# A mixture-of-experts kernel: transposes in the free quarter of the gate's PSUM bank, and down projections over two banks

## The reference

```
logits = normed @ router_w.T;  probs = softmax(logits);  top_v, top_i = top_k(probs, 2)
gates = softmax(top_v);  comb = sum over both of one_hot(top_i, 8) * gates
for e in range(8):
    gate, up = split(normed @ gate_up_w[e].T, 2)          # 384 columns each
    out = out + comb[:, e] * ((silu(gate) * up) @ down_w[e].T)
out = out + swiglu(normed, shared weights)                # 128 columns
```

## Time and profile before

| | |
|---|---|
| three runs | 674.36 us median (671.52 to 675.77) |
| profiled execution, span of the core | 674.1 us |
| profiled execution's own time | not given apart from the span; the span is 0.3 us under the median |
| mean granted TensorE clock | 0.926 |
| PE busy | 527.7 us (78%) |
| DVE, POOL and ACT busy | 391.4, 353.9 and 337.5 us |
| idle time of PE before parts 3, 0 and 1 | 36.4, 31.3 and 1.5 us |

### The profile page before, as it was taken

One profiled execution on the slowest core, in us unless ns is written; L12 is line 12 of the kernel. 1 busy time (PEld: TensorE's weight loads), 2 busy tenths in 40 slices (PEclk: granted clock), 3 DMA queues, 4 the chain that ended last, 5 costly groups with the idle time before them and its releaser, 6 DMA issues.

```text
span 674.1 us, 15456 instructions
## 1 busy us (share of the span) xinstructions
PE 527.7 (78%) x3928; PEld 472.9 (70%) x3928; DVE 391.4 (58%) x1785; ACT 337.5 (50%) x816; POOL 353.9 (52%) x515
## 2 busy tenths in 40 slices
PE   3756888787789998978896259696789887899882
PEld 2535777677778897867784258676578777899872
DVE  5576655531164886974894768678768351222454
ACT  3534444363344876744865158474554463454431
POOL 1445556565664346555274704546567666555332
PEclk9878999999998999999997669988699898999987
DMA  6915545465575454663220453411354665676894
GB/s 199 301 33 189 187 161 191 160 232 190 197 266 186 173 185 154 224 209 133 99 91 33 121 172 113 152 72 67 133 178 160 214 187 194 229 247 226 284 303 148
DMA packets 88019, 117.88 MB, mean 175 GB/s; under 512 B 11848, under 2 KB 60880, under 8 KB 87936
## 3 DMA queue, kind: packets, MB, share of 16 engines
q1 hardware_dynamic: 76208, 96.75, 42.6%
q0 software_dynamic: 9312, 19.16, 8.2%
q10 hardware_dynamic: 2416, 0.99, 0.6%
HBM read 26.57 MB, written 26.19 MB: 78 GB/s over the span
## 4 chain that ended last, share of the span: by engine, by line
PE 43%; issue 13%; DVE 12%; ACT 10%; another core or an unknown queue 9%; DMA 4%; POOL 4%; SPq 2%; ACTq 1%; DVEq 1%; POOLq 0%
PE ps_y L731 10%; PE ps_g L717 8%; PE ps_h L722 5%; PE ps_u L722 4%; DVE xres L1307 2%; PE w L629 2%; PE w L659 2%; PE ps_x L711 2%; PE w L660 2%; POOL rows L1539 2%; DMA xin<-rows 2%; PE w L615 1%; ACT zz L844 1%; PE w L675 1%
## 5 line engine op out<-in xcount | busy, mean ns | idle before, releaser
L1567 POOL DMA_INDIRECT results<-raw_gu,idx x163 | 159.6, 979 | 188.2 <-ACT raw_gu L940 127.2
L731 PE MATMUL ps_y<-dn_t,raw_gu 128*128 x978 | 145.9, 287 | 36.4 <-ACT raw_gu L940 27.0
L731 PEld LDWEIGHTS ps_y<-dn_t,raw_gu 128*128 128x128 f32 x978 | 126.2, 197 | 48.1 <-issue 47.0
L1539 POOL DMA_INDIRECT rows<-zz,s_idx x128 | 125.4, 979 | 42.6 <-issue 34.1
L717 PE MATMUL ps_g<-x_t,raw_dn 128*128 128x128 f32 x978 | 141.9, 283 | 1.5 <-issue 1.5
L717 PEld LDWEIGHTS ps_g<-x_t,raw_dn 128*128 128x128 f32 x978 | 127.5, 199 | 3.6 <-issue 3.4
L940 ACT COPY raw_gu<-ps_y 128x128 f32<-128x128 f32 x163 | 42.9, 263 | 148.1 <-PE ps_y L731 70.2
L1380 DVE TENSOR_TENSOR raw_gu<-sil,ps_u 128x384 f32<-128x384 f32 x82 | 45.2, 551 | 91.3 <-PE ps_u L722 26.6
L934 ACT ACTIVATE sil<-ps_g 128x384 f32<-128x384 f32 x163 | 80.0, 491 | 35.7 <-PE ps_g L717 17.8
L930 ACT ACTIVATE x_t<-ps_x,bf_c,gf_c 128x128 f32<-128x128 f32 x163 | 75.3, 462 | 42.6 <-PE ps_x L711 32.3
L1380 DVE TENSOR_TENSOR raw_gu<-sil,ps_h 128x384 f32<-128x384 f32 x81 | 44.7, 552 | 84.5 <-PE ps_h L722 27.5
(11 more groups left out here) (166 smaller groups left out, 747.4 us busy)
## 6 DMA issues: line engine op xcount, KB each, us to landing
raw_dn<-gu_t SPq DMA_DIRECT2D x163, 384.0 KB
xin<-rows SPq DMA_DIRECT2D x163, 64.5 KB
yg<-results SPq DMA_DIRECT2D x15, 512.0 KB
results<-raw_gu,idx POOLq DMA_INDIRECT x163
rows<-pads SPq DMA_DIRECT2D x40, 64.5 KB
rows<-pads SPq DMA_DIRECT2D x5, 451.5 KB
rows<-zz,s_idx POOLq DMA_INDIRECT x128
out<-xres SPq DMA_DIRECT2D x7, 256.0 KB
```

Of the source, the lines that this page charges most:

```text
L731: t = pe.matmul(ps_y[:, 0, :], h_t[:, k4, c * P:(c + 1) * P], dn[:, bass.ds(off + c * D, D)], start=(c == 0), stop=(c == FC - 1))
L1539: pool.indirect_dma_start(xs, bass.IndirectOffsetOnAxis(s_idx[n][:, c, k:k + 1], 0), zz[n][:, k, c, :], None).then_inc(scat[n], 16)
L1567: pool.indirect_dma_start(yt, bass.IndirectOffsetOnAxis(idx[:, ky:ky + 1], 0), yb[:, ky, :], None).then_inc(yst[ky], 16)
```

## The change

The bank `ps_x` is gone, and a second bank for the down projection takes its place. A block's rows are turned into the fourth quarter (`FC` is 3) of the bank that its gate projection uses later. The transpose therefore waits until the silu of block B-2 has read that bank, and the gate projection no longer has that wait itself. The down projection alternates between `ps_y0` and `ps_y1`, and waits for the copy of block B-2's where it waited for that of block B-1. The order of parts and the woven counts are as before. The banks that the weights are turned through at the start keep their order.

```diff
-        ps_x, ps_y = bank("ps_x"), bank("ps_y")
+        ps_y0, ps_y1 = ps_ys = bank("ps_y0"), bank("ps_y1")
         w0, w1 = bank("w0"), bank("w1")
-        weight_banks = ps_g[0], ps_u, ps_h, ps_x, ps_y, ps_g[1]
+        weight_banks = ps_g[0], ps_u, ps_h, ps_y0, ps_y1, ps_g[1]
...
-                    pe.wait_ge(xT_sb, B + 3)
+                    pe.wait_ge(sil_done, B + 3)
                     pe.wait_ge(xin_ld[k4], (B - k4) * 4 + 16)
-                    pe.transpose(ps_x[:, 0, :], xin[:, k4, 0:D], ident[:]).then_inc(xT_ps, 1)
+                    pe.transpose(ps_g[k][:, FC, :], xin[:, k4, 0:D], ident[:]).then_inc(xT_ps, 1)
                 elif part == 1:
                     pe.wait_ge(xT_sb, B + 4)
-                    pe.wait_ge(sil_done, B + 3)
                     pe.wait_ge(ws_ld[k4], (B - k4) * 4 + 16)
...
                     pe.wait_ge(h_done, B + 6)
-                    pe.wait_ge(y_sb, B + 6)
+                    pe.wait_ge(y_sb, B + 5)
...
-                        t = pe.matmul(ps_y[:, 0, :], h_t[:, k4, c * P:(c + 1) * P], dn[:, bass.ds(off + c * D, D)],
+                        t = pe.matmul(ps_ys[k][:, 0, :], h_t[:, k4, c * P:(c + 1) * P], dn[:, bass.ds(off + c * D, D)],
...
-                    act.activation(x_t[:, k, :], ps_x[:, 0, :], ACT.Identity, bias=bf_c[:], scale=gf_c[:]).then_inc(xT_sb, 1)
+                    act.activation(x_t[:, k, :], ps_g[k][:, FC, :], ACT.Identity, bias=bf_c[:], scale=gf_c[:]).then_inc(xT_sb, 1)
...
-                    act.copy(yb[:, ky, :], ps_y[:, 0, :]).then_inc(y_sb, 1)
+                    act.copy(yb[:, ky, :], ps_ys[k][:, 0, :]).then_inc(y_sb, 1)
```

## The result

The changed kernel takes 683.49 us (median of 4 runs, 681.2 to 686.26), the kernel before 673.83 (median of 4, 671.52 to 675.77). The ratio is 1.0165, with a 95% interval from 1.012 to 1.021: slower by 1.65%, some 10 to 11 us. The profiled execution took 686.26 us, its span is 684.4.

The account below looks back on a forecast made before the run. PE was taken to lead, busy 78% of the span, yet standing still about 146 us. The sum was 674.4 - 9.5 + 13.4 = 678.3, with half a microsecond for POOL's side 679 us; range 664 to 693.

Parts of the forecast that it names:

- forecast A: Whole kernel: gain and loss nearly cancel, the loss a little larger; 672 to 684 us, 679 in the middle; chance 0.45.
- Part 2: Transposes moved into the gate's bank wait for the silu of two blocks back: 13.4 us lost, bounds 0 to 29.5.
- step (b): Late silus before transposes up to 125 us: PE's gaps for other work hide the lateness, taking 12.1 us off the loss.
- Part 1: Two banks for the down projections, each waiting for an earlier block's copy: 9.5 us gained, bounds 0 to 36.4.
- C: Rival, faster: down projection stalls go and the transpose's wait stays hidden; 660 to 667 us; chance 0.17.
- B: Rival, slower: the transposes' silu waits are not absorbed, attention stages wait behind them; +20 us, 694; chance 0.28.
- D: Rival, nothing changes: the waits on PE only change their name; 674.4 us; chance 0.07.
- E: Rival, the clock: longer stops before transposes put 20 us of PE's work at the lower clock; 689 us; chance 0.03.
- Waits for ACT before D: Sign: PE's down projections' waits for ACT's copy of the result should fall from 27.0 to under 8 us.
- T(27) right behind S(25): Sign: PE's transpose of block 27 should follow ACT's silu of block 25 at once.
- The limit for B: Sign of the not-absorbed rival: idle times before down projections and transposes together growing by over 12 us.
- POOL's half microsecond: POOL's copying of row numbers after later transposes: half a microsecond added to the sum.

Follow-up runs that it names:

- its own control: Kernel before, with the silu reading a weight tile in SBUF in place of the gate's result, all waits as they were: ratio 0.9987.

## Why the prediction was right, and where it was not

**The sign and the place were right.** I gave 679 us; it is 683.5, at the upper edge of forecast A (672 to 684), and the range of 664 to 693 holds it. Slower by over 1% had 0.40, and no change that can be told had 0.44, so the outcome was not the one that I had given most. The loss is the wait of the transpose for the silu.

**Part 2, the cost: right in size.** The sum had 13.4 us. The pair that differs in this wait alone gives 1.75%, 12 us, 5 us uncertain. In detail the steps did less well. Silu waits were to be 20 to 35 us and are 42.2. Of step (b), that all lateness up to 125 us is covered, the profile shows no more than a part: T(2) waited 4.1 us, and T(6) starts 7.4 us late, 4.3 of it behind the late start of T(0). Later gaps cover more than I had counted, the wait of T(85) for its rows above all. That the steps miss and the sum fits is in part luck.

**Part 1, the gain: this step was not borne out.** "I take 9.5, the count by rows" is the term that looks mis-sized. With T's old wait it measured nothing, 0.4% slower with 0.6% uncertainty, beside its own control. There T's wait for X took 13.7 us of the idle time back, since X stands on ACT behind the same copies; I had not expected that, and had expected 9.5 us or more. In the change itself T waits for the silu, behind that X on ACT, and what the bank gave there is open: 0.6% of gain against the kernel with the transpose moved alone, 0.9% uncertain, which is 4 us and leaves room for 0 and for 9.5. With 0 in place of 9.5 the sum is 674.4 + 13.4 = 687.8; with the 12 us measured it is 686.4, 3 us above the median.

**The rivals.** C, faster with T's wait hidden, gave 664.9; with the wait truly gone the kernel came to 1.003 of before, 676 us by that ratio. So even its best case was not there. B said that the loss would not be absorbed, 694; it was absorbed about as far as the sum of 13.4 had it. D, that the waits only change their name, is right for part 1 where T kept its old wait. E, the clock: the mean granted clock fell from 0.926 to 0.902, but PE's busy time rose by 2.4 us only. PE's busy time moved by 5.8 us between two kernels with the same matmuls (both banks and the old wait beside its control), which is the size of a term, and had none in my sum; that the clock makes it is not shown.

**What was named as signs.** Waits for ACT before D under 8 us: 1.3. Idle time before T of 50 or more: 76.6. G's idle time near 1.5: 1.0. PE busy at 528: 530.1. T(27) right behind S(25), T(21) behind the table load: both, by 0.06 and 0.05 us. The limit for B, both idle times growing by over 12 us, was just not reached, with 11.5, so that sign decides little.

**POOL's half microsecond.** In the change itself POOL's waits for transposes did not grow taken together: those of the row numbers rose from 21.7 to 27.1 us, those of the scatters fell from 20.1 to 14.9. What they cost was not measured.

**What stays open.** Late silus have two causes, table loads and PE's late signals, and their shares are not separated. For that the change itself would have to run on a chip with no late signals. What part 1 gives beside the new wait, why the later copies on ACT cost 17 us, and what the changed order gives on one chip are open too.

## What to carry to other kernels

Before a second buffer is paid for with a new wait, write down for the engine that was stalled which of its waits comes last next, the old ones included: if they all hang on one in-order queue of another engine, the buffer may move the stall and not shorten it, as it did here with the old wait. Parking data in the free part of a buffer ties it to that buffer's reader, and it matters how early in the engine's order the new wait stands. Behind the gate projection the transpose's silu waits fell from 42.2 to 10.2 us and the gate's waits for X grew from 1.0 to 30.4, which still left a ratio of 1.0054 in place of 1.0165; but the two ratios come from two chips. A sum of waits made on one chip holds for that chip: compare versions within one.

## What the hardware showed that was not expected

PE's signals are late on some chips and not on others. I took each copy out of the down projection's bank (Y) before which ACT was already free when D should have ended. In the kernel before there are 109; half start within 0.04 us of D's modelled end, but 25 start over 0.5 us late, up to 3.1 us, 42 us in all. All profiles of the first and the second chip have such late copies (at least 4 of 24) and 11 or more kinds of waits for "remote", 100 to 162 us in all. The four of the third chip have none later than 0.04 us and no wait for "remote". Here is the timeline of the kernel before without exponentials on that chip, PE and then ACT:

```profile
136.62 0.27 PE L711 MATMUL ps_x<-ident,xin 128*128 128x128 f32 x1
136.73 0.83 PE L717 MATMUL ps_g<-x_t,raw_dn 128*128 128x128 f32 x6
137.40 0.83 PE L722 MATMUL ps_h<-x_t,raw_dn 128*128 128x128 f32 x6
138.07 0.83 PE L731 MATMUL ps_y<-dn_t,raw_gu 128*128 x6
138.74 0.27 PE L711 MATMUL ps_x<-ident,xin 128*128 128x128 f32 x1
...
138.94 0.27 ACT L940 COPY raw_gu<-ps_y 128x128 f32<-128x128 f32 x1 [0.85 <-PE ps_y L731]
```

A block takes 2.12 us (136.62 to 138.74) without a stop, and Y starts 0.04 us behind D's end at 138.90. Undisturbed blocks take that on the first chip too, where T(25) starts at 150.53 and T(26) at 152.67; but T(27) follows at 156.21, 5.7 us for two blocks, which take 4.2 here. Over all blocks the median from one transpose to the next is 3.11 us there and 2.56 here. In this kernel without exponentials the copies make D wait 3.8 us, not 27.0, so there is almost nothing for a second bank to win; the kernel before as it stands has no profile on this chip. It is 11% faster there (597.0 against 671.6), and PE's busy time without exponentials is 504.7 us in place of 527.7. Whether the late signals make all of that difference, and what makes them late, the profiles don't say. A late signal is itself read from the late start of the copy behind a modelled end.
